# Expert outputs scattered to token order, combine stage reading rows in order, and a new table of places

## What is computed

```
x = x + layernorm(attn(layernorm(x)))
    attn: mamba (in_proj, causal conv of 4 taps, silu, x_proj, softplus(dt),
          h[t] = exp(delta*A)*h[t-1] + delta*B*u;  y = sum_n h*C  (512 channels, 16 states),
          gate, out_proj), layernorm, q/k mixing with a gate G, projection,
          layernorm, feed-forward 256-1024-256 with gelu, layernorm
x = x + layernorm(ffn(layernorm(x)))
    ffn, for each token: dot with 8 expert embeddings, top 2, softmax over the two
         an expert takes its first 2048 tokens in token order (capacity), the rest is dropped
         out = sum over its experts of weight * (relu(tok @ W1[e]) @ W2[e])
```

## Time and profile before

| | us |
|---|---|
| median of 3 runs | 6693.94 |
| the profiled execution | 6735.03 |
| its span | 6733.1 |
| PE busy | 5418.0 |
| DVE busy | 5240.0 |
| POOL busy | 4435.8 |
| ACT busy | 3841.4 |

### The profile page before, as it was taken

One profiled execution on the slowest core, in us unless ns is written; L12 is line 12 of the kernel. 1 busy time (PEld: TensorE's weight loads), 2 busy tenths in 40 slices (PEclk: granted clock), 3 DMA queues, 4 the chain that ended last, 5 costly groups with the idle time before them and its releaser, 6 DMA issues. The chain is left out here.

```text
span 6733.1 us, 71525 instructions
## 1 busy us (share of the span) xinstructions
PE 5418.0 (80%) x16640; PEld 2989.0 (44%) x16640; DVE 5240.0 (78%) x6883; ACT 3841.4 (57%) x6622; POOL 4435.8 (66%) x2993
## 2 busy tenths in 40 slices
PE   4788888888888888888888888898888887699400
PEld 1344444444444444444444444444444444466300
DVE  4898888988898989888888888888888984111255
ACT  3566666666666666666666666666666653111255
POOL 2677777777777777777777777777777775100375
PEclk8898999998998989888998999989998987799755
DMA  7666666666665666666666666666666563122342
GB/s 254 220 222 215 218 215 214 222 217 217 217 220 208 220 217 218 214 205 205 212 211 205 211 210 210 205 211 210 206 208 215 200 207 100 50 87 87 96 145 87
DMA packets 492099, 1297.88 MB, mean 193 GB/s; under 512 B 59310, under 2 KB 216624, under 8 KB 490560
## 3 DMA queue, kind: packets, MB, share of 16 engines
q1 hardware_dynamic: 440960, 1219.82, 53.8%
q10 hardware_dynamic: 26048, 38.95, 1.7%
q0 software_dynamic: 24576, 33.72, 1.6%
HBM read 1206.19 MB, written 119.54 MB: 197 GB/s over the span
## 5 line engine op out<-in xcount | busy, mean ns | idle before, releaser
L509 POOL TENSOR_TENSOR st<-st,C_rows 128x1024 f32<-128x1024 f32 x1024 | 2486.2, 2437 | 794.0 <-DVE st L1078 790.5
L1078 DVE TENSOR_TENSOR_SCAN st<-dA,drive 128x1024 f32<-128x1024 f32 x1024 | 2339.8, 2285 | 201.5 <-ACT dA L718 67.1
L885 PE MATMUL y<-st,ident 128*128 128x512 f32 x4096 | 2138.7, 663 | 350.6 <-POOL st L509 342.4
L718 ACT ACTIVATE dA<-delta,a_neg 128x511 f32<-128x511 f32 x2048 | 1372.1, 713 | 849.4 <-DVE st L1078 723.3
L885 PEld LDWEIGHTS y<-st,ident 128*128 128x128 f32 x4096 | 832.2, 210 | 1416.6 <-issue 922.0
L1050 DVE TENSOR_TENSOR drive<-du,B_rows 128x1024 f32<-128x1024 f32 x1024 | 1259.7, 1230 | 112.3 <-DMA B_rows<-bc_rows 28.4
L1458 POOL DMA_INDIRECT rows<-expert_out,idx_c x256 | 267.3, 1044 | 626.0 <-DVE idx_c L1505 555.2
L859 PE MATMUL pre_bank<-e_abs,in_w 128*128 128x512 f32 x1024 | 565.9, 691 | 77.5 <-DVE u L1027 74.6
L838 PE MATMUL post_bank<-d_w,gT 128*128 128x256 f32 x2048 | 453.7, 380 | 27.4 <-issue 26.6
L596 POOL DMA_INDIRECT expert_in<-tb,idx x256 | 257.1, 1004 | 311.8 <-DVE idx_all L1233 235.6
L838 PEld LDWEIGHTS post_bank<-d_w,gT 128*128 128x128 f32 x2048 | 388.0, 190 | 111.6 <-issue 60.2
(11 more groups left out here) (203 smaller groups left out, 8103.6 us busy)
## 6 DMA issues: line engine op xcount, KB each, us to landing
B_rows<-bc_rows SPq DMA_DIRECT2D x1024, 512.0 KB, 3.8
C_rows<-bc_rows SPq DMA_DIRECT2D x1024, 512.0 KB, 5.2
xin<-in_x SPq DMA_DIRECT2D x32, 512.0 KB, 7.1
expert_in<-gT ACTq DMA_DIRECT2D x8, 2048.0 KB, 27.5
xn_rows<-xin SPq DMA_DIRECT2D x32, 512.0 KB, 6.2
h<-xn_rows SPq DMA_DIRECT2D x32, 512.0 KB, 7.5
x_res<-in_x SPq DMA_DIRECT2D x32, 512.0 KB, 6.4
x_rows<-x_res SPq DMA_DIRECT2D x32, 512.0 KB, 6.5
```

What stands on the lines that cost most here:

```text
L509: pool.tensor_tensor(tile[:, :, :], tile[:, :, :], bc[1][k % ROWS[1]][:, :, :], ALU.mult)\
L718: return act.activation(dA[k % 2][:, j, 1:L], delta[par][:, c, 1:L], ACT.Exp, scale=a_neg[:, c, n:n + 1])
L885: last = pe.matmul(Y[:, :], ident[:, :], st[k % RING][:, j, :], start=pair == 0 and j == 0, stop=pair == CU - 1 and j == 1)
L1078: dve.tensor_tensor_scan(st[k % RING][:, :, :].rearrange("p a l -> p (a l)"), dA[k % 2][:, :, :].rearrange("p a l -> p (a l)"), DR[:, :, : ...
```

## The change

- `expert_in` rows are 264 wide instead of 256: the token row in `tb` is followed by its two weights, its two experts (as floats) and its token number minus 2^20. The statistics of the routing are written straight into `tb`. `w_all` and `idx_all` are gone.
- A new DRAM tensor `rank_rows` has two rows for each token, one for its first and one for its second choice. It has to be zero where nothing is written: SP issues one DMA of 1 MB for each sequence in `pre`, from a zero tile of 512 columns.
- Expert stage: DVE compares the two expert numbers of each slot with the current one, picks the weight and the destination row (5 small operations, `slots_meta`), and copies the PSUM to O scaled by the weight (4 operations instead of 2). POOL scatters O with 4 indirect DMAs to `rank_rows`. SP also loads x1 of one sequence in each block into `x1_all`, which holds all 32.
- Combine stage: SP loads both rows of every token of a sequence in order (1 MB, runs of 4 KB), PE adds them with four identity matmuls of 512 columns into PSUM, DVE takes statistics from PSUM, POOL computes the reciprocal root (`pow`), ACT normalises in PSUM, DVE adds `x1_all`, ACT issues the store. Eight row buffers and four PSUM tiles are in flight.
- Gates are a stage of their own with places 30, 56 and 77. All lists `at` are new, on every engine.

The core of the diff:

```diff
-    xe_dram = nc.dram_tensor("expert_in", (NSLOT, D), F32, kind="Internal").ap()
+    DW = D + 8
+    xe_dram = nc.dram_tensor("expert_in", (NSLOT, DW), F32, kind="Internal").ap()
+    yr_dram = nc.dram_tensor("rank_rows", (2 * NTOK, D), F32, kind="Internal").ap()
# SP, pre
-                at = iter((2, 26, 56, 93))
+                at = iter((2, 13, 52, 59, 95))
+                zero_row = zeros[:, :].unsqueeze(1).to_broadcast([P, 2 * TT * D // zeros.shape[1], zeros.shape[1]])
+                sp.dma_start(yr_zero_v[b].rearrange("p (a r) -> p a r", r=zeros.shape[1]), zero_row)\
+                    .then_inc(rank_rows_zeroed, 16)
# POOL, late (the last eight are the scatters)
-                at = iter((5, 5, 19, 25, 26, 31, 31, 43, 43, 43, 43, 43, 43, 43, 43))
+                at = iter((0, 7, 18, 22, 22, 27, 29, 43, 43, 45, 46, 46, 47, 48, 49))
# DVE, late
-                at = iter((15, 18, 19, 20, 42, 42, 43))
+                at = iter((13, 18, 18, 19, 40, 40, 42))
# DVE, scan
+            def gates(b, par):
+                at = iter((30, 56, 77))
+                for c in range(KI - 1):
+                    yield next(at)
...
+                    gate(b, par, c)
-                def chunk_done(k):
-                    if k % CU == 2 and k > CU:
...
-                        gate(b, par, k // CU - 1)
-                run_slots(stages, (chunk_done, recur, ahead))
+                run_slots((gates(b, par), *stages), (nothing, recur, ahead))
# expert stage, SP
+                    for part in range(XL):
+                        at = (i * NB + n) * XL + part
+                        sp.dma_start(x1_all[:, bass.ds(at, 1), :, :], x1_wide_v[bass.ds(at, 1)]
+                                     .rearrange("s p t d -> p s t d")).then_inc(x1_loaded, 16)
# expert stage, ACT
-                    act.wait_ge(*e_out.at(n, i))
-                    act.dma_start(ye_v[i * NB + n], O[n % 2][:, :, :]).then_inc(stored[n % 2], 16)
# expert stage, POOL
+                    pool.wait_ge(*e_out.at(n, i))
...
+                    for tile in range(TB):
+                        pool.indirect_dma_start(
+                            out=yr_dram, in_=O[n % 2][:, tile, :], in_offset=None,
...
+                    pool.wait_ge(stored, 16 * TB * NB * i + 16 * TB * (n + 1))
# expert stage, DVE
-                        last = dve.tensor_copy(O[n % 2][:, tile:tile + 2, :],
-                                               OB[tile // 2][:, :].rearrange("p (a d) -> p a d", a=2))
+                        last = dve.tensor_scalar(O[n % 2][:, tile, :],
+                                                 OB[tile // 2][:, (tile % 2) * D:(tile % 2 + 1) * D],
+                                                 w_slot[:, tile:tile + 1], None, ALU.mult)
# combine stage, new
+                sp.dma_start(rows[n][:, :, :, :], yr_v[G * i + n]).then_inc(rows_loaded[n], 16)
...
+                pe.wait_ge(*(c_out.at(n - H, i) if n >= H else c_out.at(n - H + G, i - 1)))
+                for half in range(TT // 2):
+                    for c in range(2):
+                        last = pe.matmul(total[n % H][:, 2 * half:2 * half + 2, :].rearrange("p t d -> p (t d)"), ident[:, :],
...
+            turns(dve, ((2, add), (0, stats)))
+            turns(pool, ((0, scale_and_shift),))
+            turns(act, ((0, normalise), (2, store)))
```

More of the change, by code:

```diff
@@ L1334, in _ @@
                 steps.credit(act)
-            for half in range(2):
-                act.sem_inc(stored[half], 16)
             with act.Fori(0, NE // 2) as i:
@@ L1432, in _ @@
         def _(sp):
[L1433 to L1434 removed]
             def load(n, i):
[L1437 removed]
+                sp.wait_ge(*c_sum.at(n, i - 1))
                 sp.sem_inc(carried_sp_c, 1)
[L1439 to L1444 removed]
@@ L1446, in _, with add @@
-            turns(sp, ((3, store), (0, load)))
-            for n in range(G):
-                sp.wait_ge(out_stored[n], 16 * (S // G + 1))
+                sp.dma_start(rows[n][:, :, :, :], yr_v[G * i + n]).then_inc(rows_loaded[n], 16)
+            turns(sp, ((0, load),))
+        @block.tensor
+        def _(pe):
+            c_sum.credit(pe)
+            def add(n, i):
+                pe.wait_ge(rows_loaded[n], 16 * (i + 1))
+                pe.wait_ge(*(c_out.at(n - H, i) if n >= H else c_out.at(n - H + G, i - 1)))
+                for half in range(TT // 2):
+                    for c in range(2):
+                        last = pe.matmul(total[n % H][:, 2 * half:2 * half + 2, :].rearrange("p t d -> p (t d)"), ident[:, :],
+                                         rows[n][:, c, 2 * half:2 * half + 2, :].rearrange("p t d -> p (t d)"),
+                                         start=c == 0, stop=c == 1)
+                last.then_inc(c_sum.did(n), 1)
+            turns(pe, ((0, add),))
@@ L1450, in _ @@
         @block.gpsimd
         def _(pool):
[L1452 to L1461 removed]
+            c_shift.credit(pool)
@@ L1463, in _ @@
+            turns(pool, ((0, scale_and_shift),))
         @block.scalar
         def _(act):
-            for steps in (c_scaled, c_r, c_normed):
-                steps.credit(act)
-            def scaled(n, i):
-                act.wait_ge(gathered[n], 16 * 2 * TT * (i + 1))
-                act.wait_ge(*ready.at(n, i))
-                for tile in range(TT):
-                    last = act.activation(rows[n][0][:, tile, :], rows[n][0][:, tile, :], ACT.Copy,
-                                          scale=w_c[n][:, tile, 0:1])
-                last.then_inc(c_scaled.did(n), 1)
@@ L1477, in power @@
[L1477 to L1487 removed]
+            c_normed.credit(act)
```

310 lines of the change are left out of this document (178 added, 132 removed).

## The result

The changed kernel takes 6425.44 us (median of 4 runs, 6411.64 to 6459.55) where the kernel before, in the same rounds on the same chip, takes 6692.72: ratio 0.9608, 95% interval 0.9567 to 0.9649. Forecast were 6232, with a range of 6110 to 6400. The kernel is faster, as said, but by 267 us and not by 462; the time lies 25 us above the range and next to the first rival, "the scan gives nothing back, say 6430".

The account below looks back on a forecast made before the run. It took DVE's recurrence chain to bound attention, PE the expert stage, nothing full in combine. From the profiled 6735.0, -210 attention, +2 start, +5 expert, -259 combine gave 6273; 41 less for the median: 6232 us, range 6110 to 6400.

Parts of the forecast that it names:

- the scan gives nothing back: Rival, attention stage: projection or another step waits as long as the gate did; say 6430 us, chance 17%.
- Combine stage: Last stage: 156 us against 415.5, so -259, at a period of 4.2 us with four limits of 3.5 to 3.8.
- the rival of the lower clock: Combine stage: PE stays at its lower clock and limits at 7.6 us a period; 6337 us, chance 10%.
- Expert stage and its end: Expert stage: PE stays the limit, DVE's and POOL's additions are hidden, only the last block shows: +5 us.
- Start: Kernel start: three more constants and slightly longer zeroing, partly under the loads: +2 us.
- Attention stage: Scan: new order removes DVE waits, -7 us for each of 30 sequences, -210 in sum.
- the walk: Attention stage, recurrences 14 to 19: 9.8 us of DVE idle time goes, 3 returns, gain 6.8 a sequence.
- the early part of the scan: Attention stage, places not followed one by one; with the decays, 0.7 us of ACT's 1.7 waits taken as gain.
- DVE's chain: Attention stage: the recurrence on DVE is the chain; what counts is DVE's 19.3 us idle per sequence.
- The step at the gate: Attention stage: scatters split three, four and one, so the gate's 5.9 us wait per sequence falls under 1.
- The wait at the projection: Attention stage: the projection becomes late next, and DVE waits 3 us there for PE.
- Zero fill: Attention stage: 1 MB of zeros per sequence, 2.5 us ahead of a B load; 0.5 us added.

Follow-up runs that it names:

- E6: Kernel before with only the changed kernel's new slot tables and gates as an own stage: 6712.05 us, ratio 0.9986.
- the third group of runs: Runs on the third chip, where a 26-sequence stretch of the changed kernel is set beside one with two PE products halved.
- E3: Changed kernel with POOL's eight row scatters together at slot 43: 6405.49 us, ratio 0.953.
- E12: Changed kernel with the eight scatters together and each sequence's zero fill in four quarters: 6406.14 us, ratio 0.9575.
- E18: Changed kernel with ScalarE's copy at slot 35, the eight scatters together and the zero fill in quarters: 6378.22 us, ratio 0.9514.
- E14: Changed kernel with ScalarE's copy of the transposed routing rows moved from slot 36 to 35: 6375.71 us, ratio 0.9477.
- E2: Changed kernel with VectorE's query product and what follows moved from slot 44 to 41: 6461.92 us, ratio 0.9611.
- E4: Changed kernel with all slot tables of the kernel before: 6462.12 us, ratio 0.9614.
- E7: Changed kernel with the 1 MB zero fill issued twice per sequence, the second into an unread spare tensor: 6477.44 us, ratio 0.9635.
- E9: Changed kernel with PE's query product and second flow product cut to half their inner dimension (wrong outputs): 6475.24 us, ratio 0.9669.
- E17: E14 with six useless filler products on PE ahead of the third normalisation: 6355.09 us, ratio 0.9478.
- E13: Changed kernel with useless matmuls (12 and 5) in two idle stretches of PE per sequence: 6446.2 us, ratio 0.9582.
- E1: Changed kernel with one operand of VectorE's query product and score difference read from PSUM (wrong outputs): 6387.42 us, ratio 0.9495.

## Why the prediction was wrong, point by point

- **Combine stage, right in mechanism, size 19 us off.** Forecast 156 us with a range of 150 to 165, measured 137.1. The period I took, 4.2 us, was a mark-up for four limits that disturb each other. DVE's last additions give the one that came:

```profile
L1566 DVE TENSOR_TENSOR x_all<-total,x_all x32: 1195/1224/1226, 6293.2 to 6408.1; 128x1024 f32 x24, 128x1024 f32<-128x1024 f32 x8
```

  (6408.1 - 6293.2) / 31 = 3.7, which is 15 of the 19 us; the fill of 17.8 instead of 21 is most of the rest. The window above gives DMA 1.00 at 411 GB/s and PE 97%, and 1.57 MB at that rate are 3.8 us. The limits did not add. In that window PE's granted clock is 1.00, so the rival of the lower clock is out. The figure of the Trainium skill cited there (DMA: Bandwidth & Descriptors, section Where 436 GB/s comes from), 358 GB/s between HBM and SBUF, is passed by this window of one core, reads and writes together.
- **Expert stage and its end, right.** +5.4 against +5, block additions hidden at PE 98%.
- **Start.** The first recurrence starts at 105.2 instead of 98.2 us: +7, forecast +2.
- **Attention stage, wrong: -7 us a sequence forecast (-210 in the sum), -1.6 measured by the period, and 11 us in all for the new slots by themselves (E6).** It is the sum of the walk that failed, in three places. *First*, the walk added up idle time and took DVE's busy time as given. 26 sequences of the kernel before:

```profile
579.92:5106.96 4527.04, 3988.11 (x12063) 2155.67 (x12064) 4004.03 (x5019) 2885.75 (x4967) 3387.17 (x2211) 0.91 0.63 213
```

  Against the row of the changed kernel in the third group of runs, DVE's idle time fell from 20.1 to 15.0 a sequence, 5.1 of the 6.8 that the walk promised, but its busy time rose from 154.0 to 157.1, by the product's and the difference's standing ((108.3 - 38.0 + 22.7 - 5.1) / 26 = 3.4). *Second*, "the early part of the scan, which I can't follow one by one" was booked with 0.7 gained at the decays; it has 3.1 of new waits, and the decays cost 2.2 instead of 1.7. *Third*, it held DVE's chain to be the limit. E3, E12 and E18 take 2.6 us of standing away and get some 0.7, 1.1 and nothing; E14 takes nothing from DVE's work, brings one copy of ScalarE forward, and gets 1.2 to 1.9 by the traces and 1.6 to 1.8 by the medians. The reading that fits them is that several chains are about equally late, joined by waits both ways, and a gain on one is worth what the next leaves of it; no run isolates these chains.
- **The step at the gate, right in mechanism:** 5.9 us a sequence to 0.9, POOL's scatters in groups of three, four and one. The price of that very grouping was the multiply between the scatters, which caught the product.
- **The wait at the projection, wrong:** 3 forecast, 0.2 measured. It is there when the scatters or the product move (2.0 for PE in E2, 1.0 for SyncE in E3).
- **Zero fill:** +0.5 booked; the waits for B rows fell from 23.9 us to 4.6, and E4 shows no price. A second megabyte costs 1.5 us a sequence (E7).
- **The rival whose number came out,** "the scan gives nothing back", had 17%. For it stood that all places are new, and I put the walk of 35 us out of 173 against it. Its mechanism came true in part only: no step waits as long as the gate did, DVE's idle time did fall by 5.1, and what took the gain back is 3.4 us of standing inside two instructions, which no rival had.

Open: which chain is the latest at each place of the sequence, and what the lower clock costs. E9 shows that less work on PE can cost 0.5 to 0.7%, with more time at the lower clock; E17 shows that more time at the higher clock gains little or nothing at one place, and E13 gains nothing with fillers that were too long. The two are not yet one account.

## What to carry to other kernels

Before moving GpSimd's work, list the VectorE instructions whose operands both lie in SBUF, and see which GpSimd instruction will now stand beside each: they stand still as busy time, not as idle time, and a mean that more than doubles for one shape is the sign. When an engine's idle time is under a tenth of the period and a second engine is as full, do not count a removed wait at its full length until one experiment with the order alone has been timed: here 2.6 us less of standing gave between nothing and 1.1. A number moved by one slot on an engine that is nowhere the limit (ScalarE, 65% busy; its copy) was worth more than all the new slots together.

## What the runs showed of the hardware

- An instruction of four numbers (the square in E1) takes 1.89 us beside a GpSimd multiply of 128x1024, and 0.16 without; beside GpSimd's indirect DMAs the products of 128x256 keep 0.42.
- A cast of 128x8, which has one operand only, in SBUF, stands as well (0.76 us in E1 against 0.16 in the changed kernel).
- The product that stands is recorded as started 0.59 us ahead of the multiply's recorded start (3080.94 and 3081.53): the records don't tell which came first.
- One core moves 411 GB/s with all 16 engines' share at 1.00 over 80 us, two parts reads to one part writes.
- The changed kernel's time differs by 0.1% between two chips on which the kernel before differs by 0.45%.
